# A five-stage network on one core: state-space prologues reordered, and the third stage's ternary weights prepared inside the last state-space chunk

## The reference, cut to what matters

```
x = x + L0_conv(_gn(x)) ; x = x + L1_conv(_gn(x))   # two scans
t = _to_tokens(x)                                    # 1024 tokens x 512
t = t + L2_attn(_ln_t(t))                            # two Mamba-2 layers
t = t + L2_ffn(_ln_t(t))                             # Hadamard, 4-bit activations, ternary weights
t = t + L3_attn(_ln_t(t))                            # one gated state-space layer
t = t + L3_ffn(_ln_t(t))                             # 8 experts, the best 2 of each token
```

```
scale_w = clip(mean(|w|, axis=1), 1e-5)
tern = where(w/scale_w > 0.5, 1, where(w/scale_w < -0.5, -1, 0))
xh = x @ H ; s = clip(max|xh|, 1e-5)/7 ; xq = clip(round(xh/s), -8, 7)*s
out = xq @ (tern*scale_w).T
```

## Time and profile before

| | us |
|---|---|
| median of 3 runs (lowest, highest) | 1483.61 (1482.70, 1485.13) |
| the profiled execution: its own time | 1482.89 |
| its span in the trace | 1480.9 |
| busy: PE, DVE, ACT, POOL | 1243.8, 1013.0, 762.9, 277.8 |
| mean granted TensorE clock, share of full | 0.913 |

### The profile page before, as it was taken

The page is one execution under the profiler, slowest core; times in us unless marked ns, Lnnn a source line. Parts: engine busy times, 40 slices in busy tenths (PEclk is TensorE's granted clock), DMA queues, the critical chain, the costliest instruction groups (busy, mean ns, idle before and its releaser), DMA issues.

```text
span 1480.9 us, 33586 instructions
## 1 busy us (share of the span) xinstructions
PE 1243.8 (84%) x12394; PEld 858.4 (58%) x12395; DVE 1013.0 (68%) x1671; ACT 762.9 (52%) x1228; POOL 277.8 (19%) x347
## 2 busy tenths in 40 slices
PE   4734889998677999847489999768999999998996
PEld 2204666674566767524255555546677677767674
DVE  3567788888778888958766666476557765476432
ACT  2316667677566776622644334334466655375331
POOL 0120233323123333311100000025111111111111
PEclk9766999999899999979789999658999999999998
DMA  4024000002200000121220000328446564446111
GB/s 146 1 87 189 12 6 6 4 4 88 95 11 7 4 4 5 60 118 54 96 115 1 0 0 0 119 72 277 157 135 240 188 217 135 142 165 220 22 27 21
DMA packets 38016, 120.25 MB, mean 81 GB/s; under 512 B 9848, under 2 KB 14072, under 8 KB 27968
## 3 DMA queue, kind: packets, MB, share of 16 engines
q1 hardware_dynamic: 32304, 107.28, 20.0%
q0 software_dynamic: 5648, 12.13, 4.0%
HBM read 105.61 MB, written 12.76 MB: 80 GB/s over the span
## 4 chain that ended last, share of the span: by engine, by line
PE 67%; DVE 14%; ACT 9%; issue 5%; DMA 2%; POOL 2%; DVEq 0%; ACTq 0%; POOLq 0%; SPq 0%
PE banks L2273 15%; PE banks L2294 15%; PE banks L1075 10%; PE banks L1804 6%; PE banks L1834 3%; ACT mb_ca L829 2%; DVE mb_ca L633 2%; PE banks L1207 2%; PE banks L1167 1%; PE banks L1157 1%; DVE mb_M L682 1%; PE banks L1100 1%; PE banks L2243 1%; PE banks L339 1%; DVE sq L259 1%
## 5 line engine op out<-in xcount | busy, mean ns | idle before, releaser
L2273 PE MATMUL banks<-eb_x_hi,eb_w_hi 128*128 128x128 f16 x1344 | 228.5, 220 | 4.6 <-DVE eb_w_lo L2153 4.6
L2273 PE MATMUL banks<-eb_x_lo,eb_w_hi 128*128 128x128 f16 x1344 | 228.5, 220 | 0.0
L2273 PE MATMUL banks<-eb_x_hi,eb_w_lo 128*128 128x128 f16 x1344 | 228.5, 220 | 0.0
L1075 PE MATMUL banks<-mb_u_hi,mb_wi_hi 128*128 (+3 forms) x1088 | 190.6, 221 | 13.8 <-ACT mb_ca L829 11.0
L1075 PE MATMUL banks<-mb_u_hi,mb_wi_lo 128*128 (+3 forms) x1088 | 190.4, 221 | 0.0
L1075 PE MATMUL banks<-mb_u_lo,mb_wi_hi 128*128 (+3 forms) x1088 | 190.2, 221 | 0.0
L2153 DVE TENSOR_TENSOR eb_w_lo<-eb_raw,eb_w_hi 128x2048 f32 (+1 forms) x64 | 142.6, 2286 | 23.0 <-ACT eb_w_hi L2159 16.1
L633 DVE SCALAR_TENSOR_TENSOR mb_ca<-mb_xp,mb_par,mb_ca 128x128 f32<-128x128 f32 x384 | 149.0, 449 | 5.3 <-ACT mb_ca L829 3.4
L2273 PEld LDWEIGHTS banks<-eb_x_hi,eb_w_hi 128*128 128x128 f16 x1344 | 132.4, 98 | 7.3 <-issue 5.0
L2273 PEld LDWEIGHTS banks<-eb_x_lo,eb_w_hi 128*128 128x128 f16 x1344 | 132.3, 98 | 2.4
L2273 PEld LDWEIGHTS banks<-eb_x_hi,eb_w_lo 128*128 128x128 f16 x1344 | 132.4, 98 | 0.0
(11 more groups left out here) (443 smaller groups left out, 2835.8 us busy)
## 6 DMA issues: line engine op xcount, KB each, us to landing
eb_raw<-e_w SPq DMA_DIRECT2D x64, 1024.0 KB, 6.2
mb_ring<-m_in_w SPq DMA_DIRECT2D x8, 1072.0 KB, 5.2
ab_raw<-a_in_w SPq DMA_DIRECT2D x4, 1154.0 KB, 12.0
mb_ring<-m_out_w SPq DMA_DIRECT2D x4, 1024.0 KB, 5.3
xcm<-x_cm SPq DMA_DIRECT2D x4, 512.0 KB, 5.1
t_res<-x_tm SPq DMA_DIRECT2D x1, 2048.0 KB, 9.1
t_kept<-t_res SPq DMA_DIRECT2D x1, 2048.0 KB, 8.4
mb_wi_hi<-t_kept SPq DMA_DIRECT2D x1, 2048.0 KB, 8.8
```

Of the source, the lines that this page charges most:

```text
L1075: x = e.matmul(ps[0:width, bank, n * P:(n + 1) * P], a[:, k, f:f + width], b[:, k, ds(i * P, P)], start=(k == 0 and m == 0), stop=(k == KD ...
L2273: o = e.matmul(ps[:, j, c * P:(c + 1) * P], a[:, side, k, f * P:(f + 1) * P], b[:, k, :], start=(k == 0 and m == 0), stop=(k == KD - 1 and ...
```

## The change

Five things are done, and the SBUF areas of `stage_ffn` and `stage_l3` are laid out so that the early buffers are free.

1. **First prologue.** `kept` is written tile by tile at the end of `stage_l01`, and the first two weight pieces are issued there too (`sp_ahead`). DVE no longer overwrites `t` first: it makes `lower(0, 0)` and `lower(0, 1)` while POOL computes the two roots, normalises once with their product, and writes the rows `h` later (`first_rows`).
2. **First chunk of each layer.** PE makes two differences ahead of its transposes; ACT makes `upper(l, 5)` and silu(B, C) earlier, half of silu(x) later, and the exponentials of the sums after the third `E`.
3. **Last chunk's squares** are summed by POOL, for both layers, and PE adds one matmul between the halves of `out_project`. DVE's `row_norm` of it comes later.
4. **Third stage's weights.** SP loads them and the Hadamard matrix after `kept` (back); DVE, PE and ACT make, turn and copy them in and after the last chunk of layer 2. POOL instead of DVE adds `kept`, and DVE only takes statistics.
5. **Third stage** begins with a power on POOL in place of ACT's root and DVE's reciprocal.

```diff
@@ stage_l01, sp
         e.dma_start(t[:], ins["x_tm"]...)
+        for i in range(TT):
+            e.wait_ge(added_odd if i % 2 else added, TT // 2 + i // 2 + 1)
+            e.dma_start(core.kept[:, i, :], t[:, i, :]).then_inc(core.t_kept, 16)
@@ stage_mamba, sp
+    def sp_ahead(e):
+        for n in range(2):
+            e.dma_start(raw[n], W_IN[0, n * P:(n + 1) * P, :]).then_inc(raw_in[n], 16)
...
-        e.dma_start(kept, t[:]).then_inc(t_kept, 16)
-        piece(0, 0)
-        piece(0, 1)
...
         e.dma_start(back, kept).then_inc(t_back, 16)
+        core.ffn.load(e)
@@ stage_mamba, dve
         aggregate(0, TT)
+        lower(0, 0)
         e.wait_ge(rstd_done, 1)
-        e.wait_ge(t_kept, 16)
-        for i in range(TT):
-            x = e.tensor_scalar(h[:, i, :], t[:, i, :], mv[:, i, 0:1], rstd[:, i:i + 1], ALU.subtract, ALU.mult)
-        own(x)
-        own(e.tensor_tensor(rstd[:], rstd[:], rstd[:], ALU.mult))
+        own(e.tensor_copy(rstd1[:], rstd[:]))
+        own(e.tensor_tensor(rstd[:], rstd1[:], rstd1[:], ALU.mult))
         own(e.tensor_tensor(mv[:, :, 1], mv[:, :, 1], rstd[:], ALU.mult))
-        own(e.memset(mv[:, :, 0], 0.0))
         e.tensor_scalar(rstd[:], mv[:, :, 1], MB_EPS, None, ALU.add).then_inc(var_done, 1)
+        lower(0, 1)
+        e.wait_ge(rstd_done, 2)
+        own(e.tensor_tensor(rstd[:], rstd[:], rstd1[:], ALU.mult))
...
             if l == 0:
-                e.wait_ge(rstd_done, 2)
                 normalise(range(TT))
-                lower(0, 0)
-                lower(0, 1)
... (after the split of the rows and lower(0, 3))
+                e.wait_ge(core.t_kept, 16 * TT)
+                first_rows(range(6))
... (after dtn)
+                first_rows((6, 7))
@@ last chunk of layer 2, dve, after M
-                    e.wait_ge(t_back, 16)
-                    whole((0, 1, 2))
+                    core.ffn.scales(e)
+                    core.ffn.weights(e, 0)
... (after from_state, next_state)
-                        whole((3,))
+                        core.ffn.weights(e, 1)
@@ after the last chunk, dve: layer 1
-                row_norm(last)
                 e.wait_ge(rstd_done, 3)
                 e.wait_ge(ysq_done, last + 1)
                 normalise(range(4))
                 lower(l + 1, 2)
                 lower(l + 1, 3)
+                row_norm(last)
@@ layer 2
+                core.ffn.weights(e, 2)
+                core.ffn.weights(e, 3)
+                whole_stats(range(TT - 1))
                 row_norm(last)
-                whole((4, 5, 6))
-                own(e.tensor_tensor(h[:, TT - 1, :], h[:, TT - 1, :], back[:, TT - 1, :], ALU.add))
+                e.wait_ge(sum_done, TT)
                 add_rows(TT - 1, last)
@@ stage_mamba, act
+            upper(l, 5)
             e.wait_ge(sums_mm, l + 1)
             e.activation(sums[0:MB_CR, P:TOK], ...)
-            upper(l, 5)
...
-            silu_x(l * TT, True)
+            silu_bc(l * TT, True)
+            silu_half(l * TT, 0)
...
             project_z(l * TT, 0)
-            (dend, edec: the exponentials of the sums)
+            silu_half(l * TT, 1)
... (in the first chunk, after the third E)
+                        decay_sums()
... (after the last chunk of layer 2)
+                core.ffn.evacuate(e, 0)
+                core.ffn.evacuate(e, 1)
             upper_y(l * TT + TT - 1)
             square_y(l * TT + TT - 1)
+                core.ffn.evacuate(e, 2)
+                core.ffn.evacuate(e, 3)
+                core.ffn.evacuate_scale(e)
@@ stage_mamba, pool, last chunk of layer 2
+                    e.wait_ge(t_back, 16)
+                    e.wait_ge(h_done, LAYERS * TT - 2)
+                    add_kept(range(TT - 2))   # t = h + back, six tiles
                 if not is_first:
                     power(g - 1)
                 (yi = yi + dx)
+                    e.wait_ge(h_done, LAYERS * TT - 1)
+                    add_kept((TT - 2, TT - 1))
             chunks(e, l, body)
-            e.sem_inc(ysum_done, 3)
+            sum_squares(l * TT + TT - 1)
@@ stage_mamba, pe
+                if is_first:
+                    e.wait_ge(pairs_in, (1 + MB_SPLIT) * 16 * (g + 1))
+                    differences(0)
+                    differences(1)
... (in the first chunk project_x follows differences 2 to 5, not 1 to 4)
             chunks(e, l, body)
-            e.wait_ge(ysq_done, (l + 1) * TT)
-            for j in range(JD):
-                x = e.matmul(ps[:, 2, 384:385], ysq[:, j, :], core.ones[:, 0:1], ...)
+            if l + 1 == LAYERS:
+                core.ffn.turn(e, 0)
+                core.ffn.turn(e, 1)
             out_project(l * TT + TT - 1, 0, JD // 2)
             ...
+            sum_rows(l * TT + TT - 1)
             out_project(l * TT + TT - 1, JD // 2, JD)
+                core.ffn.turn(e, 2)
+                core.ffn.turn(e, 3)
+                core.ffn.spread(e)
@@ stage_ffn, pool
+        e.memset(mhalf[:], -0.5)
         e.memset(minus_magic[:], -FF_MAGIC).then_inc(magic_set, 1)
+        e.wait_ge(magic_set, 1)
+        e.wait_ge(var_done, 1)
+        e.tensor_tensor(rstd[:], rstd[:], mhalf[:], ALU.pow).then_inc(rstd_done, 1)
```

More of the change, by code:

```diff
@@ L401, in stage_mamba @@
     cum = sb("cum", [MB_CR, TOK], F16)
+    ring = sb("ring", [P, 2 * MB_DPROJ])
+    raw = [ring[:, b * MB_DPROJ:(b + 1) * MB_DPROJ] for b in range(2)]
     pairs = sb("pairs", [P, H2 * P], F16)
@@ L744, in body, with whole_stats @@
                 e.tensor_tensor(y, y, sz[:, side, :, :], ALU.mult).then_inc(y_done, 1)
-            def whole(tiles):
+            def whole_stats(tiles):
                 for i in tiles:
-                    own(e.tensor_tensor(t[:, i, :], h[:, i, :], back[:, i, :], ALU.add))
+                    e.wait_ge(sum_done, i + 1)
                     e.bn_stats(core.stats[:, i, :], t[:, i, :])
@@ L1012, in power, with add_kept @@
                 e.tensor_tensor(rs[:], rv[:], mhalf[:, 0:1], ALU.pow).then_inc(pow_done, 1)
+            def add_kept(tiles):
+                for i in tiles:
+                    e.tensor_tensor(t[:, i, :], h[:, i, :], back[:, i, :], ALU.add).then_inc(sum_done, 1)
             conv_bc(l * TT)
@@ L1143, in pe, with differences @@
             e.wait_ge(fixed_in, 3 * 16)
+            def differences(k):
+                e.matmul(ps[:, 3 + k % 2, :], tails[:, k, :], pairs[:, 512 * k:512 * k + 512], start=True, stop=True)\
+                    .then_inc(diff, 1)
             def body(i, g, is_first, is_last, side):
+                if is_first:
+                    e.wait_ge(pairs_in, (1 + MB_SPLIT) * 16 * (g + 1))
+                    differences(0)
+                    differences(1)
                 e.wait_ge(c0_in, (g + 1) * 16)
@@ L1278, in rounds, with load, scales, weights @@
                     step(r - lag)
-    def sp(e):
-        e.dma_start(wn[:], ins["f_w"].rearrange("(j p) i -> p j i", p=P)).then_inc(w_in, 16)
-        e.dma_start(had[:], ins["c_had"].rearrange("(k p) n -> p k n", p=P)).then_inc(had_in, 16)
+    class Ahead:
+        def load(self, e):
+            e.dma_start(wn[:], ins["f_w"].rearrange("(j p) i -> p j i", p=P)).then_inc(w_in, 16)
+            e.dma_start(had[:], ins["c_had"].rearrange("(k p) n -> p k n", p=P)).then_inc(had_in, 16)
+        def scales(self, e):
+            self.own = Chain(e, tern_own)
+            e.wait_ge(w_in, 16)
+            self.own(e.tensor_reduce(asum[:], wn[:], AX.X, ALU.add, apply_absolute_value=True))
+            self.own(e.tensor_scalar(scale[:], asum[:], 1.0 / D, FF_QEPS, ALU.mult, ALU.max))
+            e.tensor_scalar(half[:], scale[:], 0.5, None, ALU.mult)
+            self.own(e.tensor_scalar(nhalf[:], scale[:], -0.5, None, ALU.mult))
+        def weights(self, e, j):
+            e.tensor_scalar(diag[:, j, :], core.ident[:], scale[:, j:j + 1], None, ALU.mult)
+            if j >= 2:
+                e.wait_ge(tern_done, j - 1)
+            self.own(e.tensor_scalar(low[:, j % 2, :], wn[:, j, :], nhalf[:, j:j + 1], None, ALU.is_lt))
+            e.scalar_tensor_tensor(out=tern[:, j, :], in0=wn[:, j, :], scalar=half[:, j:j + 1], in1=low[:, j % 2, :],
+                                   op0=ALU.is_gt, op1=ALU.subtract).then_inc(tern_done, 1)
+        def turn(self, e, j):
+            e.wait_ge(tern_done, j + 1)
+            for k in range(KD):
+                x = e.transpose(ps[:, FF_TURNED_TO[j], k * P:(k + 1) * P], tern[:, j, k * P:(k + 1) * P], core.ident[:])
+            x.then_inc(w_tr, 1)
+        def spread(self, e):
+            for j in range(KD):
+                x = e.matmul(ps[:, 5, j * P:(j + 1) * P], core.ones[:], diag[:, j, :], start=True, stop=True)
+            x.then_inc(wsc_mm, 1)
+        def evacuate(self, e, j):
+            e.wait_ge(w_tr, j + 1)
+            e.activation(ternT[:, :, j * P:(j + 1) * P], ps[:, FF_TURNED_TO[j], :].rearrange("p (k c) -> p k c", k=KD), ACT.Copy)
+        def evacuate_scale(self, e):
+            e.wait_ge(wsc_mm, 1)
```

(13 more changed lines are left out.)

147 lines of the change are left out of this document (74 added, 73 removed).

## The result

| | before | after |
|---|---|---|
| median, us | 1483.15 (1481.53 to 1485.13, 4 runs) | 1472.18 (1470.02 to 1474.03, 4 runs) |
| after / before | | 0.9925, 95% interval 0.9905 to 0.9945 |
| span of the profiled execution, us | 1480.9 | 1469.3 |
| mean granted clock | 0.913 | 0.912 |

The changed kernel is 11.0 us faster; predicted were 14.2.

What follows compares the result with a forecast made beforehand. The prediction took the kernel as PE-bound on average (67% of the chain), the change touching only stretches where it is not. Terms -5.9 - 4.4 - 3.9 = -14.2 took 1482.89 to 1468.7, median 1469.4; range 1464 to 1476.

Steps and rivals of the forecast that it cites:

- rival (a): End of layer 2 and third stage: POOL's adds, collision with y and colder out_project use up the gain; 1473.3, chance 0.14.
- rival (b): Prologues give half: late start costs 2.6, h writes delay dt, pace catches up; -5 instead of -10.3, 1474.7, chance 0.10.
- first prologue, to `la` (A): First prologue: normalisation 1.0 earlier, ACT's 2.44 wait gone, dt projection at 134.2 not 137.31; two h writes make `la` 0.5 late.
- first chunk, layer 1 (B): Layer 1's first chunk: reorder brings the last M to 164.8 from 170.67, 5.9 earlier with the prologue's gain included.
- layer boundary (F): End of layer 1: out_project starts once y_lo is there, ending at 390.0 not 391.29; gain 1.3, bounds 0 and 2.5.
- first chunk, layer 2 (G): Layer 2's first chunk: same reorder without the prologue, last M at 430.3 instead of 433.40, 3.1 earlier.
- last chunk to y_lo (C): Last chunk of layer 2: POOL's adds delay `power`, slipping the end 2.4; adds beside y times silu(z) cost 0.6 more.
- y_lo to the opening (D): End of layer 2: y_lo at 643.8, out_project to 653.3, stage opens at 656.4 against 653.8.
- third stage (E): Third stage: third tile's amax 22.7 after opening instead of 30.4, 7.7 less, with the power waiting behind POOL's semaphore clearing.
- table in stage four: Fourth stage: its root must now load its own table, on the path, costing 1.28.
- Rival (c): Third stage: PE runs cold, a tile needs 7.3, and the kernel gets slower; 1486.3, chance 0.05, of which 0.02 is slower.
- (d): Expert stage: changed rounding adds or drops a block, 21.5; 1490.9 or 1447.9, chance 0.03 up, 0.02 down.

Runs made afterwards that it cites:

- after_again: The changed kernel, unchanged, timed again on another chip; ratio to the kernel before 0.9919 (0.9902 to 0.9935).
- e4: Kernel before with only the third stage's early weights, POOL's adds of kept and its root as a POOL power; ratio 0.9996 (0.9985 to 1.0007).
- e6: Changed kernel with POOL's eight adds of kept left out, so later stages see other data; ran once, 1445.4 us with one expert block fewer.
- e7: Changed kernel with `lower(0, 1)` moved behind the normalisation in the first prologue; ratio to the kernel before 0.9909 (0.9891 to 0.9927).
- e1: Kernel before with only the first prologue's part of the change; ratio 0.9988 (0.9977 to 0.9999), 1.8 us faster.
- e2: Kernel before with only the new order of the first chunk of each layer; ratio 0.996 (0.9946 to 0.9974), 5.9 us faster.
- e3: Kernel before with only the last chunk's squares moved from PE to POOL, both layers; ratio 0.9983 (0.9973 to 0.9993), 2.5 us faster.
- e9: Changed kernel with PE making the eight x transposes of each first chunk twice; ratio to the kernel before 0.9957 (0.9944 to 0.997).
- e10_both: Changed kernel with third stage's root back on ACT and DVE, and `lower(0, 1)` behind the normalisation; ratio to the kernel before 0.9861 (0.9845 to 0.9876).
- e11_chunk_end: e10_both with all four weight blocks after y_lo and four of POOL's adds after its sum with dx; ratio to the kernel before 0.985 (0.9834 to 0.9866).
- e5: Changed kernel with the third stage's root back on ACT and its reciprocal on DVE; ratio to the kernel before 0.9891 (0.9875 to 0.9907).

## Why the prediction was nearly right

Predicted was a gain of 14.2, measured were 11.0. Direction and range hold, but the time alone, 1472.2, does not choose between the forecast (1469.4), rival (a) (1473.3) and rival (b) (1474.7); the stretches do. Step by step, against the table:

| step | predicted | measured | |
|---|---|---|---|
| first prologue, to `la` (A) | -2.6 | -1.5 | second root blocked |
| first chunk, layer 1 (B) | -3.3 | -1.8, -3.0 in after_again | clock |
| layer boundary (F) | -1.3 | -0.7, -0.2 | turns at half clock |
| first chunk, layer 2 (G) | -3.1 | -3.0, -1.6 in after_again | right; clock |
| last chunk to y_lo (C) | +3.0 | +5.5, +5.0 | DVE blocked by POOL |
| y_lo to the opening (D) | -0.5 | -1.7 | `out_project` mis-sized |
| third stage (E) | -7.7 | -9.5, -9.3, -8.2 in e4 | clock rose sooner |
| table in stage four | +1.3 | +1.3 | right |

In C and D the table takes the prediction's terms (2.4 and 0.6). Its times read otherwise: y_lo at 643.8 is 2.5 after the 641.3 of the kernel before, and D is then unchanged. Together they are +2.5 either way; measured were +3.9.

**Where the missing 3.2 lie.** The prologues and boundary (A, B, F, G) were to give 10.3 and gave 6.9 (6.4 in after_again); the end (C, D, E, table) was to give 3.9 and gave 4.3 (4.6). The prologues are thus nearer to rival (b)'s 5 than to the forecast. Of (b)'s reasons, the late start cost 1.2 and not 2.6. The rows h did delay `la`: dt's projection starts 2.3 earlier than before (3.1 predicted), `la` ends only 1.5 earlier, so the two writes cost 0.9 where I had 0.5. The pace did not catch up: B gave 3.0 in after_again. The rest of the loss is what (b) did not name: the blocked root and the clock.

**The step that failed** is the pricing of POOL beside DVE, and it is furthest off in the last chunk: "I put 0.6 on it (0 to 1.3)" and "three small ones 0.5, one weights block 1.35". I had POOL slowed by DVE (1.45 an add). It was the other way: POOL's adds ran at 1.23 and DVE's tiny operations took up to POOL's whole duration. C cost 5.5 instead of 3.0, and e6 puts 3.6 of the 5.5 on the adds; the remaining 1.9 are the two weights blocks, the second beside POOL's sum with dx. A rule that speaks of this I had not weighed. The Trainium skill (SBUF — State Buffer, SBUF: two separate sides) says that DVE, in a two-port mode or (against a GpSimd instruction that reads SBUF) with two SBUF inputs, and GpSimd hold their shared ports exclusively, each for a whole instruction. The trace agrees: the two small operations at 620.82 and 622.10 each ended 0.03 after the add that was running; in which mode they ran, it doesn't show.

**The same in the prologue.** "the second `lower` to 114.7 with the 1.65 root under it": the root took 3.72 under it, and the normalisation started 13.6 after the statistics where I had 11.5. Of those 2.1, 1.5 is the blocked root and 0.8 a wait of the first `lower` for ACT. e7 gives 2.3 back. The start itself went better (+1.2 against +2.1), by the lower price of an issue that I had as a bound.

**The prologue's and the first chunk's gains don't add.** Compared by A plus B, and only where the clock doesn't fall: e4 has the old code of both and takes 70.0, e1 67.0, e2 67.2, after_again with both 65.7. So 3.1 and 2.8 alone make 4.3 together, not 5.9. That each alone makes ACT less late, and this can be had only once, would explain it; I did not test that. The changed kernel's own 67.1 is 1.4 more, and 1.25 of that is the chunk with the low clock.

**The boundary's** last add of rows came 1.2 earlier after y_lo, where I had 1.3. But then the clock was 0.5 from 387.3 to 390.7, PE turned the rest in that time, and DVE's splits follow those.

**The end** was right by offsetting errors, which is luck. From the last M to the fourth stage's statistics 5.6 are gained, less 1.3 for the table: 4.3, against 3.9 predicted. C was 2.5 worse than priced, D 1.2 and E 1.8 better. In D the term for `out_project` was mis-sized. I had it done 9.5 after y_lo (5.1 cold, that is at half clock, 0.6 for the squares, 3.8 for a second half that is half cold), against 10.8 in the kernel before, "having been warmed by the squares". It was done 8.1 after y_lo in the changed kernel and 7.8 in e3: the second half took 2.8 at full clock and the summing 0.2. The squares had not warmed that first half in the kernel before either (e3), so taking their 3.6 away cost nothing in clock. Rival (a), "the end gives nothing", can't be excluded for parts 4 and 5 alone (e4: 0.6 faster, interval 2.2 faster to 1.0 slower); for the whole end the columns speak against it.

**Rival (c)** did not come true in any execution of the changed stage. In the changed kernel the clock rises within the first rotation, whose eight matmuls take 2.48 (1.90 at full clock), and stays up until 701.3. How soon it rises belongs to the execution too: it was 11.4 after the opening in the changed kernel and 14.3 in e4, whose first rotation ran cold throughout and whose E is 1.2 longer. So up to 1.2 of the 1.8 that E gave beyond the forecast is luck. **(d)** didn't happen, and e6 shows its price.

**What stays open.** Stages four and five have the same code in before, e1, e2 and e3, and took 763.8, 765.4, 767.4 and 761.6: 5.9 apart. A difference of two profiles below that says nothing there, so the 1.6 that the changed kernel lost there beside the table load is unexplained and may be nothing. e9's slower median is unexplained too, and so is which idle time of PE a clock fall follows.

The best kernels run are e10_both and e11_chunk_end, 1461.8 and 1461.2 against 1482.3 before. They can't be told apart; e10 is the smaller edit, and both beat the changed kernel.

## What to carry to other kernels

When work is moved onto an idle engine, ask not only if it fits there but which other engine's instructions it will block: here POOL's adds were cheap and DVE's smallest operations paid for them. Put such work beside an engine that waits, or where DVE reduces or reads PSUM. A root of a stage's first rows belongs on an engine that has nothing in front of it: POOL's came 4.5 after its input, because POOL cleared 75 semaphores first, and the order of work of each queue from the stage's opening on has to be counted. And run the same program twice before a clock fall is given a cause.

## What the runs showed of the hardware

- **DVE beside POOL, both on SBUF.** A DVE operation on [128, 4] took 1.25 (0.17 alone), one on [128, 128] 2.34 (0.28 in e6), ending within 0.1 of POOL's. The other way, POOL's root on [128, 8] took 3.72 under a `lower` and 1.65 alone (e7). An instruction that is small waits as long as the other engine's running one takes.
- **Not all DVE operations pay.** The reduction (2.29 in e6 without adds and 2.29 beside them) and M, which reads PSUM (two in 1.27 without adds and 1.28 beside them), did not.
- **Where the granted clock falls differs between executions of one program.** In two of them a first chunk had a fall to 0.5 at 155 in one and at 417 in the other, and was 1.25 and 1.36 longer than without; in e5, with a fall at 157, it was 2.1 longer.
- **Clearing semaphores on POOL takes time.** 75 clears, one every 0.064, took 5.1 at the opening of the third stage, and the power behind them waited.
- **An issue of a 1 MB load by SP took 0.47** (two in 0.94), and 0.90 each where they stood behind the 2 MB write. Whether the large write was the reason, no run separates.
